# Self-attention output product: one fp32 product, or three passes of rounded operands, on one Trainium2 core

## What is computed

```python
def _attn(xq, xc, Wq, Wk, Wv, Wo, bo):
    q, k, v = heads(xq @ Wq), heads(xc @ Wk), heads(xc @ Wv)
    attn = softmax(einsum('bnhd,bshd->bhns', q, k) * 64 ** -0.5)
    out = einsum('bhns,bshd->bnhd', attn, v).reshape(B, N, 1024)
    return out @ Wo + bo
x = _attn(_ln(x, g1, b1), _ln(x, g1, b1), Wq1, Wk1, Wv1, Wo1, bo1) + x   # this part
x = _attn(_ln(x, g2, b2), context, Wq2, Wk2, Wv2, Wo2, bo2) + x
x = _geglu_ff(_ln(x, g3, b3), Wp, bp, Wf, bf) + x
```

## Time and profile before

| | before |
|---|---|
| median of three runs | 1501.79 us (1500.88 to 1502.48) |
| profiled execution, whole | 1503.09 us |
| its span, first to last instruction | 1501.3 us |
| PE busy (matmul) | 1400.0 us, 93% |
| DVE busy | 924.5 us, 62% |
| ACT busy | 871.4 us, 58% |
| POOL busy | 351.2 us, 23% |
| mean granted TensorE clock | 0.981 |
| part A | 0 to 306.5 us |

### The profile page before, as it was taken

How to read it: one execution, slowest core, us unless ns; L and a number is a source line. 1 busy time by engine, 2 the same in 40 slices (tenths; PEclk the granted TensorE clock), 3 DMA queues, 4 the chain that set the end, 5 groups by cost and what they waited for, 6 DMA issues and landing times. The chain is left out here.

```text
span 1501.3 us, 30424 instructions
## 1 busy us (share of the span) xinstructions
PE 1400.0 (93%) x12018; PEld 1185.4 (79%) x12018; DVE 924.5 (62%) x1734; ACT 871.4 (58%) x2424; POOL 351.2 (23%) x522
## 2 busy tenths in 40 slices
PE   6999999978999999999999988997899999998797
PEld 5787878767888888888888877997677777776687
DVE  3647473748766776787678764444566666676442
ACT  3637373755655555566556654443577767776554
POOL 1011010031211121122111100001565756563000
PEclk9999999999999999999999997999899999999899
DMA  9000000002000000000000002000100000000000
GB/s 248 16 1 2 1 1 1 2 29 101 9 9 9 9 9 9 9 9 12 6 9 17 2 1 85 1 0 15 28 17 10 17 17 18 17 10 2 1 25 25
DMA packets 25069, 30.27 MB, mean 20 GB/s; under 512 B 1409, under 2 KB 22881, under 8 KB 24673
## 3 DMA queue, kind: packets, MB, share of 16 engines
q1 hardware_dynamic: 24928, 28.33, 6.5%
HBM read 26.49 MB, written 1.84 MB: 19 GB/s over the span
## 5 line engine op out<-in xcount | busy, mean ns | idle before, releaser
L839 ACT ACTIVATE B_probs<-banks,B_neg_max 112x375 f32<-112x375 f32 x256 | 143.4, 573 | 110.3 <-DVE B_neg_max L937 110.3
L1743 DVE TENSOR_REDUCE D_neg_max<-banks 112x2 f32<-112x750 f32 x128 | 114.1, 933 | 84.9 <-PE banks L1867 84.9
L1646 ACT ACTIVATE D_probs<-banks,D_neg_max 112x375 f32<-112x375 f32 x256 | 143.2, 574 | 39.7 <-DVE D_neg_max L1743 39.7
L786 POOL TENSOR_TENSOR B_q_hi<-B_q_group,ones 128x224 fp32r<-128x224 f32 x64 | 36.3, 567 | 402.4 <-PE banks L1047 354.5
L937 DVE TENSOR_REDUCE B_neg_max<-banks 112x2 f32<-112x750 f32 x128 | 114.1, 933 | 26.1 <-PE banks L1047 24.7
L643 PE MATMUL banks<-B_ctxT,B_wk_hi 128*128 128x378 f32 x384 | 115.7, 355 | 6.6 <-DVE B_wk_lo L928 4.4
L1874 PE MATMUL banks<-ident,D_probs 112*126 112x112 f32 x768 | 98.8, 265 | 8.3 <-DVE D_probsT L1748 7.0
L643 PE MATMUL banks<-B_wv_hi,B_ctxT 128*126 128x512 f32 x288 | 105.9, 421 | 0.0
L945 DVE TENSOR_SCALAR B_probs<-B_probs,B_rsums 112x375 f32<-112x375 f32 x256 | 102.0, 441 | 4.5
L954 DVE TENSOR_TENSOR B_k_lo<-banks,B_k_hi 128x378 fp32r<-128x378 f32 x128 | 69.9, 548 | 53.0 <-ACT B_k_hi L853 53.0
L1070 PE MATMUL banks<-ident,B_probs 112*126 112x112 f32 x768 | 95.5, 260 | 5.8 <-DVE B_probs L945 4.5
(11 more groups left out here) (312 smaller groups left out, 3816.4 us busy)
## 6 DMA issues: line engine op xcount, KB each, us to landing
ctx<-in_ctx_dram SPq DMA_DIRECT2D x32, 189.0 KB
ctx<-in_ctx_dram SPq DMA_DIRECT2D x32, 92.2 KB
w_stage<-in_L_xattn_Wq_dram SPq DMA_DIRECT2D x2, 1024.0 KB, 7.6
w_stage<-in_L_xattn_Wp_dram SPq DMA_DIRECT2D x1, 2048.0 KB, 7.8
w_stage<-in_L_xattn_W_dram SPq DMA_DIRECT2D x2, 1024.0 KB, 6.5
out_dram<-x_tokens SPq DMA_DIRECT2D x4, 448.0 KB, 3.2
x_tokens<-in_x_dram SPq DMA_DIRECT2D x1, 1344.0 KB, 18.8
w_stage<-in_L_xattn_Wk_dram SPq DMA_DIRECT2D x1, 1024.0 KB, 9.6
```

Of the source, the lines that this page charges most:

```text
L839: nc.scalar.activation(P[:, c, 0:S], SB[0:N, c, 0:S], ACT.Exp, bias=nm[:, c:c + 1], accum_out=sm[:, c:c + 1]).then_inc(exp_done, 1)
L1646: nc.scalar.activation(P[:, m % 2, j, 0:S], SB[0:N, j, 0:S], ACT.Exp, bias=nm[:, m % 2, j:j + 1], accum_out=sm[:, odd, 4 * m + j:4 * m + j ...
L1743: nc.vector.tensor_reduce(nm[:, m % 2, 2 * half:2 * half + 2], SB[0:N, 2 * half:2 * half + 2, 0:S], AX.X, ALU.max, negate=True).then_inc(m ...
```

## The change

The outputs and the weights of the product are kept as two rounded parts each, and the product is three passes: high by high, low by high, high by low. ACT's copy out of bank 6 now rounds (`oh`), and DVE gets a new instruction `o_rest`, which subtracts `oh` from the same bank into `ol`. It stands in DVE's queue ahead of `maxima` in the steps 2 to 7, behind `keys(0)` and `keys(3)` at the start of the next group, and twice at the end. TensorE now waits for `ol` (semaphore `o_lo`) where it waited for the copy. The weights are split once, in four pieces, during the q and k units 4 to 7 of the first group: ACT rounds (`wo_round`), DVE subtracts (`wo_rest`). The wait for the load of `Wo` moves from TensorE to ACT.

```diff
...
         PT = sb("probsT", [N, 2, 4, N])
-        oT = sb("oT", [128, NP, N])
+        woh, wol = [sb(f"wo_{n}", [128, NP, D], F32R) for n in ("hi", "lo")]
+        oh, ol = [sb(f"oT_{n}", [128, NP, N], F32R) for n in ("hi", "lo")]
         nm = sb("neg_max", [N, 2, 2, 4])
...
         rcp_done, norm_done, t_done = sem("rcp_done"), sem("norm_done"), sem("turned")
-        pt_act, pt_dve, av_done, o_out = sem("probsT_act"), sem("probsT_dve"), sem("av_done"), sem("oT_out")
+        pt_act, pt_dve, av_done, o_hi = sem("probsT_act"), sem("probsT_dve"), sem("av_done"), sem("oT_hi")
+        o_lo, wo_hi, wo_lo = sem("oT_lo"), sem("wo_hi"), sem("wo_lo")
         y_done, y_out, x_done = sem("y_done"), sem("y_out"), sem("x_done")
...
                 act.wait_ge(av_done, i + 1)
-                nc.scalar.activation(oT[:, 4 * p:4 * p + 4, :].rearrange("p u n -> p (u n)"), OB[:, 0:4 * N], ACT.Copy
-                                     ).then_inc(o_out, 1)
+                nc.scalar.activation(oh[:, 4 * p:4 * p + 4, :].rearrange("p u n -> p (u n)"), OB[:, 0:4 * N], ACT.Copy
+                                     ).then_inc(o_hi, 1)
+
+            def wo_round(c):
+                if c == 0:
+                    act.wait_ge(wo_in, 16)
+                u = slice(2 * c, 2 * c + 2)
+                nc.scalar.activation(woh[:, u, :], wo[:, u, :], ACT.Copy).then_inc(wo_hi, 1)
 
...
                     queries(g, u)
+                    if g == 0 and u >= 4:
+                        wo_round(u - 4)
                     if u == 0 and g:
...
 
+            def o_rest(i, p):
+                dve.wait_ge(o_hi, O0 + i + 1)
+                u = slice(4 * p, 4 * p + 4)
+                nc.vector.tensor_tensor(ol[:, u, :].rearrange("p u n -> p (u n)"), OB[:, 0:4 * N],
+                                        f32(oh[:, u, :]).rearrange("p u n -> p (u n)"), ALU.subtract).then_inc(o_lo, 1)
+
+            def wo_rest(c):
+                dve.wait_ge(wo_hi, c + 1)
+                u = slice(2 * c, 2 * c + 2)
+                nc.vector.tensor_tensor(wol[:, u, :], wo[:, u, :], f32(woh[:, u, :]), ALU.subtract).then_inc(wo_lo, 1)
+
             def y_evac(t):
...
                     keys(g, u)
+                    if g == 0 and u >= 4:
+                        wo_rest(u - 4)
                     if u == 0 and g:
+                        o_rest(g * STEPS, 0)
                         pt_evac(g * STEPS)
+                    if u == 3 and g:
+                        o_rest(g * STEPS + 1, 1)
                     if u == 6 and g:
...
                         y_evac(g * GB + (s - 1) // 2)
+                    if s >= 2:
+                        o_rest(i, s % 2)
                     maxima(i, s % 2)
...
             norm(NG * STEPS, 1, 1)
+            o_rest(NG * STEPS, 0)
             pt_evac(NG * STEPS)
+            o_rest(NG * STEPS + 1, 1)
             y_evac(B)
...
                 pe.wait_ge(pt_dve, PT0 + turned)
-                pe.wait_ge(o_out, i + O0)
+                pe.wait_ge(o_lo, i + O0)
                 for u in range(4):
...
             def project(i, t, p):
-                pe.wait_ge(o_out, i + O0 + 1)
+                pe.wait_ge(o_lo, i + O0 + 1)
                 if p == 0:
                     pe.wait_ge(y_out, t + Y0)
                 for u in range(4 * p, 4 * p + 4):
-                    ins = nc.tensor.matmul(YB[0:N, 0:D], oT[:, u, :], wo[:, u, :], start=(u == 0), stop=(u == NP - 1))
+                    nc.tensor.matmul(YB[0:N, 0:D], oh[:, u, :], woh[:, u, :], start=(u == 0), stop=False)
+                    nc.tensor.matmul(YB[0:N, 0:D], ol[:, u, :], woh[:, u, :], start=False, stop=False)
+                    ins = nc.tensor.matmul(YB[0:N, 0:D], oh[:, u, :], wol[:, u, :], start=False, stop=(u == NP - 1))
                 if p == 1:
...
                         lambda t: ln.hi[:, t, :], lambda t: ln.lo[:, t, :], KT).then_inc(qk_mm, 1)
-                    if n == 5:
-                        pe.wait_ge(wo_in, 16)
                     tail(first, g * GB, n)
                 pe.wait_ge(q_out, (g + 1) * NP)
                 pe.wait_ge(k_out, (g + 1) * NP)
                 scores(first, 0, 0, 0)
                 pe.wait_ge(wv_lo, 1)
-                pe.wait_ge(o_out, first + 2 + O0)
+                pe.wait_ge(o_lo, first + 2 + O0)
                 pe.wait_ge(y_out, g * GB + Y0 + 1)
...
                     i = first + s
+                    if g == 0 and s == 2:
+                        pe.wait_ge(wo_lo, 4)
                     if s == 2:
...
```

## The result

The changed kernel takes 1509.41 us (median of five runs, 1509.19 to 1510.49); the kernel before, run beside it, 1501.87 (1500.88 to 1502.69). The ratio is 1.005, with a 95% interval of 1.004 to 1.0061: slower by 7.5 us, where +11.4 was forecast. The profiled execution of the changed kernel has a span of 1507.6 us and took 1509.40 as a whole, 1.8 more, as before.

The account below looks back on a forecast made before the run. It took a loop of DVE and ACT, not PE, to bound part A's steps. Terms 13.8 - 2.5 + 0.1 = +11.4 us on the median of 1501.79 gave 1513.2 us, range 1507.5 to 1519.

Parts of the forecast that it names:

- The loop of maxima, exponentials and product: Part A's steps: DVE and ACT wait for each other, 4.70 us per plain step, with nothing of PE in it.
- PE is the bound: Rival: PE sets the pace everywhere, so the passes save 10.0 us and the kernel takes 1491.8 us; chance 0.03.
- the price of `o_rest`: Part A's steps: 0.53 us per plain step, 0.99 in step 6 of the first three groups; +13.8 us in all.
- the rivals that made `o_rest` dearer or cheaper: Waits for ACT every step, about 1523, chance 0.05; stretched by POOL, 1515, 0.05; half hidden, 1507 to 1511, 0.12.
- 21 x 0.53: Part A's steps: all but three hand on the whole start-to-start time of `o_rest`, 11.1 us.
- the projections: Starts of groups 2 to 4: PE sets the pace, so shorter half projects save 1.9 and 0.7 us, together -2.5.
- The end of part A: Last project of part A: everything stands alone, `o_rest` comes between copy and shorter project, +0.1 us.
- splitting the weights: First group's projections: four ACT copies and four DVE subtractions fit into idle time, zero cost.
- the wait that TensorE loses cost nothing, since it was met: First group's projections: moving the wait for the load of `Wo` from PE to ACT gains nothing.
- half of `o_rest` is hidden: Rival: only plain steps pay and PE covers step 2, or maxima wait for scores; +5 to +9 us, chance 0.12.
- near 318: Where part A was to end in the changed kernel's profile, in us.
- the rest shifts as a whole: Parts B to E: unchanged, only starting later, so the whole kernel moves as part A does.

Follow-up runs that it names:

- dve_only: Kernel before plus a DVE subtraction in all places of `o_rest`, into a tile nothing reads, product still fp32: part A +12.0 us, whole +10.2, ratio 1.0066.
- pe_only: Changed kernel with `o_rest` only in steps 2 and 3 of the first group, three passes kept: part A -2.4 us, ratio 0.9961 against the kernel before.
- no_rest_s7: Changed kernel without `o_rest` in step 7 of groups 1 to 3: part A 275.7 us against the changed kernel's 276.0; ratio 1.0047 against the kernel before.
- before_again: Kernel before, unedited, under a new name: part A +0.2 us, whole +0.3 us, ratio 0.9999 against the kernel before.
- tile_only: Kernel before plus one unused tile and one unused semaphore: part A 0.0 us, whole -0.6 us, ratio 0.9996.
- delay: Kernel before plus 52 idle matmuls on PE ahead of part A's last `values`: part A +9.7 us, whole +9.6 us, ratio 1.006.
- hybrid: Three passes and `o_rest` only in steps 7 of groups 1 to 3 and the two halves behind each, fp32 elsewhere: part A -1.7 us, ratio 0.9972 against the kernel before.

## Why the prediction was right or wrong

**Right: what bounds the steps.** The loop of maxima, exponentials and product set the pace, not the engine with 93%. dve_only brings the whole loss (+12.0) with every matmul of the kernel before left in place; pe_only takes the matmul time away and leaves a plain step at 4.71. The rival "PE is the bound" asked for -10 in part A and is refuted at -2.4 (-3.4 without the two `o_rest` left in it). The Trainium skill ("Perfetto Trace Analysis", Identifying the Most-Contended Engine) has the most-contended engine as the one to optimize first, but judges TensorE by the busy share of its weight loads and not by that of its matmuls. The rows agree with it so far: in the steps weight loads were busy 20.41 of 25.55 us, less than DVE's 21.11 and ACT's 21.15, and in the projections 23.74 of 28.00, far above both the earlier trace rows. The rival read the column of matmuls.

**Right: the price of `o_rest`.** 0.53 in a plain step was forecast, 0.54 measured; 0.99 for step 6 was forecast, 6.16 - 5.17 = 0.99 measured; durations of 614 to 625 ns, as part B's. Step 2 cost 0.48, so it was not covered. Of the rivals that made `o_rest` dearer or cheaper none came: it waited for ACT among the first group's steps only in step 6 (by 0.49 us), and POOL's split did not stretch it. POOL of the kernel after:

```profile
76.89 1.86 POOL L212 TENSOR_TENSOR A_xT_hi<-A_xT,ones 128x448 fp32r<-128x448 f32 x2 [15.90 <-ACT A_xT L191]
78.71 2.25 POOL L216 TENSOR_TENSOR A_xT_lo<-A_xT,A_xT_hi 128x448 fp32r<-128x448 f32 x2
```

`o_rest` at 77.89 lies beside L212 and took 0.62; `x_update` at 79.96 lies beside L216 and took 1.28, where its next instance, at 85.96 behind the split, took 0.42. As forecast, the product L434 now comes behind the split (81.36, 0.62 long), but `x_update` has come into it. The Trainium skill ("SBUF — State Buffer", SBUF: two separate sides) has VectorE and GpSimd share a port pair that a VectorE instruction with two SBUF inputs needs; these two instructions agree with it (`o_rest` has one input from PSUM and kept 0.62 us, `x_update` has two from SBUF and took 1.28), though they lie beside two different POOL instructions.

**Wrong: `o_rest` in step 7 of groups 1 to 3.** The sum said "21 x 0.53", all steps but three, as if every maxima handed its delay on. Those of step 7 do not hand it to the next group. PE of the kernel after, at the end of the first group's steps:

```profile
83.27 0.59 PE L556 MATMUL banks<-ident,A_probs 112*112 112x112 f32 x4 [0.57 <-DVE A_probs L434]
83.81 0.38 PE L575 MATMUL banks<-A_wo_hi,A_oT_hi 128*112 128x256 f32 x1
84.02 0.28 PE L576 MATMUL banks<-A_wo_hi,A_oT_lo 128*112 128x256 f32 x1
...
85.18 0.28 PE L577 MATMUL banks<-A_wo_lo,A_oT_hi 128*112 128x256 f32 x1
85.30 0.37 PE L224 MATMUL banks<-A_xT_hi,A_wq_hi 128*128 128x448 f32 x1
```

The projections (L224) stand behind the product (L575), the product behind the transposes (L556), and these wait for the product L434, which comes ahead of `o_rest` and maxima of step 7 in DVE's queue. `o_rest` (83.14 to 83.76) is ready 0.05 us before L575 at 83.81 and holds it by little: without it, in no_rest_s7, L575 starts 83.98 - 39.61 = 44.37 us behind the first maxima instead of 44.47. Counted from each kernel's first maxima, the project of step 7 starts at 82.11 - 40.69 = 41.42 before and 83.81 - 39.34 = 44.47 after: 3.05 later. Steps 2 to 6 make 0.48 + 3 x 0.53 + 0.99 = 3.06 of it; the 0.10 of waiting for `o_rest` is offset by the 0.11 that the product beside POOL's split no longer costs. Of the 0.53 of step 7 nothing is in it, while the maxima of step 7 are 3.48 later. The whole next group hangs on the project. So 3 x 0.53 = 1.6 us go out of the sum. dve_only (0.60 shorter at each border with no pass changed) and no_rest_s7 (0.3 us for all three instructions) show the same from two sides.

The end of these rows also gives the price of a pass: (85.18 - 84.02) / 10 = 0.116 apart, where part B's 0.118 was taken.

**Right in size: the projections.** Forecast -2.5. A border takes 28.98 us after, 29.71 in dve_only and 30.31 before; the passes make 29.71 - 28.98 = 0.73 of it, 2.2 in all. The end of part A, +0.1 forecast, came to +0.1 (last maxima to part B's first transpose, 12.12 before and 12.26 after); there everything stood alone, as expected:

```profile
311.68 0.62 DVE L450 TENSOR_TENSOR A_oT_lo<-banks,A_oT_hi 128x448 fp32r<-128x448 f32 x1 [2.49 <-ACT A_oT_hi L355]
...
312.36 0.37 PE L575 MATMUL banks<-A_wo_hi,A_oT_hi 128*112 128x256 f32 x1 [1.30 <-DVE A_oT_lo L450]
```

**Right: splitting the weights costs nothing.** The eight instructions, by groups (busy us, mean ns, idle before), kernel after:

```profile
L456 DVE TENSOR_TENSOR A_wo_lo<-A_wo,A_wo_hi 128x512 fp32r<-128x512 f32 x4 | 2.7, 682 | 0.0
L362 ACT ACTIVATE A_wo_hi<-A_wo 128x512 fp32r<-128x512 f32 x4 | 2.5, 624 | 0.0
```

The ACT copies took the 0.62 us of the estimate. From the first projection matmul to the first maxima it is 40.69 - 16.43 = 24.26 us before and 39.34 - 16.10 = 23.24 after; the 1.0 us between them is the slower matmuls at the start, 15 before and 9 after, each 0.17 us dearer (below). The splitting shows in neither direction. No run took it out by itself.

**Wrong, though small: "the wait that TensorE loses cost nothing, since it was met".** It was met in the one profile that the forecast had. In three of the five profiles of kernels that keep it PE stood for it: 1.12 us in before_again, 0.69 in dve_only, 0.36 in tile_only. PE of before_again:

```profile
26.21 0.47 PE L224 MATMUL banks<-A_xT_hi,A_wq_hi 128*128 128x448 f32 x1 [1.12 <-DMA A_wo<-in_L_xattn_Wo_dram]
```

The load of `Wo` lands at about 26 us, and whether PE is at its unit 5 by then varies from one execution to the next. In the seven profiles of kernels that have moved this wait PE does not wait for the load. The mean of the five waits is 0.4 us, an estimate of what moving it is worth, ahead of part A's first maxima and so outside the measure.

**The sum again.** The six steps of a group are 3.5 us longer in groups 1 to 3, of which each border gives 1.34 back: 3 x 2.18 = 6.5. Group 4 has no `act_full` and no border behind it: 3.2. With 0.1 for the end this is 9.8, which is what part A shows. With 1.6 taken out of it, the forecast's own sum would have been +9.8. The whole kernel's +7.5 also lies within the +5 to +9 of the rival "half of `o_rest` is hidden", but by coincidence: step 2, which it had covered by PE, paid its 0.48. And part A ended at 315.3 us of the profile where "near 318" was forecast, because it also began its steps 1.35 us earlier.

**Wrong or unproven: that the rest shifts as a whole.** It did so in delay, as far as its interval tells, and not in the changed kernels. In all eight series with `o_rest` or passes in them the whole moved 1.7 to 2.4 us less than part A (mean 2.1); in before_again, delay and tile_only it was -0.6 to +0.1. The traces do not settle where. Ahead of the first maxima the eight take 39.2 to 40.6 us (mean 39.8), the four of the kernel before's kind 39.9 to 40.7 (40.3); behind part A 1190.6 to 1194.3 (mean 1192.3) against 1191.6 to 1194.6 (1193.5). That would be 0.5 and 1.2 us, but two profiles of the kernel before alone lie 2.8 apart behind part A (1194.4 and 1191.6), and two of the kernel after 1.7. Ahead of the first maxima the moved wait for `Wo` accounts for 0.4 (dve_only keeps it and still moved 1.8 less). The mean granted clock of the executions explains little: over the 48 executions of the kernel before beside which the experiments were timed, 0.001 more of it goes with 0.49 us less, and the eight series have on average 0.0006 more, which makes 0.3 us (an estimate). At the start the rate of the matmuls adds a spread of its own. In the first projections, PE's timeline of the kernel before:

```profile
21.05 0.57 PE L224 MATMUL banks<-A_xT_hi,A_wq_hi 128*128 128x448 f32 x1
21.42 0.57 PE L225 MATMUL banks<-A_xT_lo,A_wq_hi 128*128 128x448 f32 x1
...
22.14 0.37 PE L224 MATMUL banks<-A_xT_hi,A_wq_hi 128*128 128x448 f32 x1
22.34 0.36 PE L225 MATMUL banks<-A_xT_lo,A_wq_hi 128*128 128x448 f32 x1
```

And of the kernel after:

```profile
19.22 0.49 PE L226 MATMUL banks<-A_xT_hi,A_wk_lo 128*128 128x448 f32 x1
19.55 0.37 PE L224 MATMUL banks<-A_xT_hi,A_wk_hi 128*128 128x448 f32 x1
```

The first matmuls of 448 columns are 0.37 us apart and last 0.57; from 22.1 us before and from 19.5 after they are 0.20 apart and last 0.36 or 0.37. PE had worked without a pause since 16.43 and 16.10. The two spacings stand nearly as the clock's two levels, 1.2 and 2.4 GHz, but the profile has the granted clock at 1.00 on both sides of the step, so it does not confirm that the clock is the cause. Six more matmuls at the wide spacing make 1.0 us between these two profiles, and the earlier start 0.3. It is not a mark of the changed kernels: the narrow spacing begins at 19.2 to 21.6 us in their eight profiles and at 19.4 to 22.1 in the four of the kernel before's kind. What makes the rest of the 2 us, some 1.4 by these estimates, stays open: no run here changed it on purpose.

## What to carry to other kernels

The matmul busy time didn't tell here which engine to relieve; the spacing of one instruction that recurs in every step did, with the list of what it waits for. Work that moved from an engine beside the loop into the loop's own queue cost its whole start-to-start time, even though the busy time of the relieved engine fell; do such an exchange only at those steps behind which the other engine sets the pace (hybrid, 9 of 32 halves, gains 1.7 us in part A, where the full exchange loses 9.8). And at the border of two stages ask which instruction the next stage stands behind: a delay behind that one is not passed on.

## What the runs showed of the hardware

The rate of TensorE at the start differs from profile to profile: matmuls of the same projections came 0.37 us apart until 22.1 us in one and 19.5 us in the other, and 0.20 apart after, with a granted clock of 1.00 in the profile throughout. Stretches of the same instructions behind part A took 1190.6 to 1194.6 us. A difference of 2 us in 1500 can't be read from a pair of profiles here.

A DVE sum of two SBUF tiles of 112 x 256 took 1.28 us beside POOL's split against 0.42 behind it, three times as long; the product in the earlier trace rows had been stretched to twice its time only. A DVE subtraction of 128 x 448 with one input from a bank kept 0.62 us beside the split.
